# Moving a bias add ahead of the next tile's row split in a one-core SSM and mixture-of-experts kernel

## The reference, cut to what matters

```python
# x: 8 x 512 tokens x 256; first block: x + layernorm(S4D convolution block of layernorm(x))
def ffn(x, ...):                       # second block, 8 experts, 2 of them per token
    z = layernorm(x) * g + b
    probs = softmax(z @ rW + rb)
    w = the two largest probs, normalised to sum 1, zero elsewhere
    hid = gelu(z @ W1[e] + b1[e])      # 256 -> 512, every expert e
    outs = hid @ W2[e] + b2[e]         # 512 -> 256
    return x + sum over e of outs * w
x = x + layernorm(ffn(layernorm(x)))
```

## Time and profile before

| | us |
|---|---|
| median of 3 runs (lowest to highest) | 584.14 (581.31 to 586.74) |
| the profiled execution | 590.15 |
| its span, first to last instruction | 588.3 |
| TensorE busy, of the span | 479.5 (82%) |
| VectorE busy | 439.7 (75%) |
| ScalarE busy | 346.2 (59%) |
| GpSimd busy | 338.8 (58%) |
| mean granted clock of TensorE | 0.936 of full speed |

### The profile page before, as it was taken

The page is one execution under the profiler, slowest core; times in us unless marked ns, Lnnn a source line. Parts: engine busy times, 40 slices in busy tenths (PEclk is TensorE's granted clock), DMA queues, the critical chain, the costliest instruction groups (busy, mean ns, idle before and its releaser), DMA issues.

```text
span 588.3 us, 11874 instructions
## 1 busy us (share of the span) xinstructions
PE 479.5 (82%) x2775; PEld 393.4 (67%) x2775; DVE 439.7 (75%) x1468; ACT 346.2 (59%) x788; POOL 338.8 (58%) x266
## 2 busy tenths in 40 slices
PE   0297899968999974977699999999999999999200
PEld 0137888757889863543498888888888888888200
DVE  6999895999889875645677777777777777777183
ACT  6991854565676575812356555555555566556265
POOL 0000559533777883672247776767677676767457
PEclk9997999999999977979799999999999999999755
DMA  6304710051335548653544444444444444444497
GB/s 159 129 1 180 287 36 1 2 169 63 116 119 189 192 146 286 243 188 113 155 92 74 74 75 69 76 75 73 71 76 74 73 75 73 73 72 59 71 401 286
DMA packets 50161, 70.38 MB, mean 120 GB/s; under 512 B 10160, under 2 KB 39728, under 8 KB 49584
## 3 DMA queue, kind: packets, MB, share of 16 engines
q1 hardware_dynamic: 34528, 51.81, 27.1%
q0 software_dynamic: 15568, 17.81, 18.3%
HBM read 37.90 MB, written 31.69 MB: 118 GB/s over the span
## 4 chain that ended last, share of the span: by engine, by line
DVE 35%; ACT 19%; issue 17%; PE 14%; POOL 4%; DMA 4%; DVEq 3%; SPq 2%; ACTq 0%; POOLq 0%
DVE hb L1089 6%; ACT z_f L625 6%; ACT yw L648 4%; PE psum L1312 4%; DVE z_hl L1081 3%; DVE z_hl L1079 3%; POOL acc L1236 3%; DVEq L299 2%; DVE st L689 2%; DMA y_rows<-yw,dst 2%; PE psum L1283 2%; PE psum L1270 2%; DVE ws L883 2%; PE psum L1259 2%; PE psum L1260 1%
## 5 line engine op out<-in xcount | busy, mean ns | idle before, releaser
L1218 POOL DMA_INDIRECT y_rows<-yw,dst x71 | 115.9, 1632 | 54.5 <-DVE widx L1074 19.8
L1418 PE MATMUL psum<-ws,z_hl 128*128 x426 | 119.4, 416 | 1.1 <-DVE z_hl L1081 1.1
L1437 PE MATMUL psum<-ws,h_hl 128*128 x852 | 115.5, 285 | 0.1
L639 ACT ACTIVATE hg<-hb 128x512 f32<-128x512 f32 x71 | 44.9, 633 | 103.8 <-DVE hb L1089 81.1
L1437 PEld LDWEIGHTS psum<-ws,h_hl 128*128 128x128 f32 x852 | 103.2, 188 | 0.3 <-issue 0.3
L1205 POOL DMA_INDIRECT wt<-w_rows,widx x71 | 70.1, 988 | 44.5 <-issue 18.4
L1418 PEld LDWEIGHTS psum<-ws,z_hl 128*128 128x128 f32 x426 | 77.5, 189 | 16.1 <-issue 1.9
L1163 POOL DMA_INDIRECT z_rows<-zn,pos x64 | 68.8, 1074 | 28.7 <-issue 17.1
L1089 DVE TENSOR_TENSOR hb<-psum,b1r 128x512 f32<-128x512 f32 x71 | 49.1, 692 | 31.0 <-issue 29.4
L1312 PE MATMUL psum<-yf,it 128*128 128x256 f32 x256 | 59.9, 390 | 2.6 <-DVE r L932 2.6
L625 ACT ACTIVATE z_f<-psum,gb 128x128 f32<-128x128 f32 x142 | 56.0, 444 | 9.3 <-PE psum L1405 8.4
(11 more groups left out here) (204 smaller groups left out, 863.3 us busy)
## 6 DMA issues: line engine op xcount, KB each, us to landing
z_in<-z_rows SPq DMA_DIRECT2D x71, 129.0 KB
w_raw<-in_dram SPq DMA_DIRECT2D x16, 512.0 KB, 5.6
xs<-in_dram SPq DMA_DIRECT2D x8, 512.0 KB, 5.7
x_dram<-xs SPq DMA_DIRECT2D x8, 512.0 KB
y_rows<-zn SPq DMA_DIRECT2D x8, 512.0 KB, 3.2
yr<-y_rows SPq DMA_DIRECT2D x8, 512.0 KB, 6.5
out_dram<-acc SPq DMA_DIRECT2D x7, 512.0 KB, 4.7
b1r<-in_dram SPq DMA_DIRECT2D x8, 256.0 KB
```

Of the source, the lines that this page charges most:

```text
L1218: pool.indirect_dma_start(y_rows, bass.IndirectOffsetOnAxis(ap=dst[m][:, 0:1], axis=0), yw[m % 3][:, :], None, compute_op=ALU.add).then_in ...
L1418: last = TE.matmul(ps_h[q], z_hl[q][:, a, k], w_at(e1, c, k * F, F), start=n == 0, stop=n == 5)
L1437: last = TE.matmul(ps_y[q], h_hl[q][:, a, k], w_at(e2, c, 1024 + k * H, H), start=n == 0, stop=n == 11)
```

## The change

In VectorE's `part`, the bias add of tile i+1 goes from behind the split of tile i+2 to the head of the part. The load of an expert number, which stood ahead of that bias add and was for tile i+1, now stands ahead of the split and is for tile i+2; the bias add takes the register that the part before has loaded.

```diff
             def part(i, par, u):
+                t, q = i + 1, 1 - par
+                if live(t):
+                    e = expert(dve, t, u + 1)
+                    dve.wait_ge(sem("l1_mm"), t + 1)
+                    if not early(t):
+                        dve.wait_ge(sem("hg_ready"), t)
+                    V.tensor_tensor(hb[:, :], ps_h[q], b1r[:, bass.ds(e, 1)].rearrange("p a f -> p (a f)"),
+                                    ALU.add).then_inc(sem("hb_ready"), 1)
                 t, q = i + 2, par
                 if live(t):
...
                     V.tensor_tensor(widx[slot(t, u, 2) % 3][:, :], z_in[q][:, H:H + 1], flag[:, :],
                                     ALU.add).then_inc(sem("dest_ready"), 1)
+
+                    expert(dve, t, u + 2)
                     dve.wait_ge(sem("zf_ready"), t + 1)
...
                     V.tensor_tensor(z_hl[q][:, 1], z_f[:, :, :], z_hl[q][:, 0].bitcast(F32),
                                     ALU.subtract).then_inc(sem("z_split"), 1)
-                t, q = i + 1, 1 - par
-                if live(t):
-                    e = expert(dve, t, u + 1)
-                    dve.wait_ge(sem("l1_mm"), t + 1)
-                    if not early(t):
-                        dve.wait_ge(sem("hg_ready"), t)
-                    V.tensor_tensor(hb[:, :], ps_h[q], b1r[:, bass.ds(e, 1)].rearrange("p a f -> p (a f)"),
-                                    ALU.add).then_inc(sem("hb_ready"), 1)
                 t, q = i, par
                 if live(t):
                     dve.wait_ge(sem("h_high"), t + 1)
```

## The result

| | before | changed |
|---|---|---|
| median (lowest to highest), us | 585.22 (581.31 to 586.74), 4 runs | 653.96 (651.33 to 655.03), 4 runs |
| the profiled execution, us | 590.15 | 651.33 |
| ratio of changed to before, 95% interval | | 1.118 (1.111 to 1.125) |

The changed kernel is 11.8% slower; 646 us were forecast, within 628 to 664. The first place to look is the line of the bias add, whose first and last start bound the loop (answers to the earlier trace rows). The second line is the load of the expert number (answers to the earlier trace rows).

A forecast was written before the change was run, and what follows sets the result against it. It took the loop to be bound by a new chain, split, first-layer product, hb, next split: terms sum to 4.51 us a tile against 3.63, 0.88 more, 62 us over 70 periods, 584 + 62 = 646 us; range 628 to 664.

The forecast's parts named there:

- Step 1: VectorE, start of the new chain: hb to the next operation 0.61 us, `row_of` to `widx` 0.43 us.
- Step 2: VectorE, `widx` to the first half of the split, with the load between: 0.72 us, bounds 0.11 and 0.83.
- a rival of 4%: Load of the expert number slow at its new place: 0.26 us more a tile, 4.77 us and 664 us; 4%.
- Step 3: VectorE, first half of the split to its second half: 0.33 us.
- steps 3 to 5: Split halves 0.33 us; second half to weight load 0.57; first-layer product on TensorE 1.65; product's end to hb 0.20.
- The wait in front of hb: VectorE would stand 1.00 us a tile ahead of hb, until the first-layer product ends.
- TensorE's share in the loop: Sign of being right: TensorE's busy share in the loop falls to some three quarters.
- The load hides: Rival: the load runs during the wait for `flag`, period 3.90 us, time 603 us; 8%.
- hb is not kept waiting: Rival: product done when VectorE reaches hb, VectorE's row of 3.51 us sets the period, 576 us; 4%.
- The clock falls: Rival: TensorE's pauses lower its clock, chain at least 1.29 us longer, 736 us or more; 3%.
- The rule on the load: Skill's floor of about 600 ns for a `tensor_load`: `widx` to split some 0.3 us longer, total near 667 us.
- TensorE's floor: TensorE's own need in the loop: 3.32 us a tile, 0.31 under the period, so at most 22 us to win.

The follow-up runs named there:

- e8: Changed kernel with GpSimd's scatter of tile t held back until hb of tile t+4 is done; 653.04 us, ratio 1.112.
- e1: Changed kernel with the load of the expert number moved from between `widx` and the split to directly behind hb; 606.73 us, ratio 1.037.
- e4: Changed kernel with three of the six first-layer matmuls left out; 598.52 us, ratio 1.021.
- e5: Kernel before with three of the six first-layer matmuls left out; 585.21 us, ratio 0.999.
- e2: Kernel before with only the load moved, from directly ahead of hb to directly behind it; 569.79 us, ratio 0.976.
- e3: Kernel before with only the load moved, to between `widx` and the split, for one tile more ahead; 576.51 us, ratio 0.985.

## Why the prediction was right, step by step

The mechanism was right, and so were the sign, the range and the order of size. Of the steps, for the mean of the tiles from 300 to 600 us:

- Step 1, hb to the next operation and `row_of` to `widx`: 0.61 + 0.43 forecast, 0.61 + 0.44 measured.
- Step 2, `widx` to the split: 0.72 forecast, 0.84 measured. This is the term that was mis-sized. Its make-up was right: with the DMA engines idle it is 0.72 to 0.73 us, and with the scatter moved (e8) 0.74 in the mean. What the forecast didn't see is that a load which begins in a certain stretch behind a scatter's start is held up, and that the new order puts it there: 43 of the changed kernel's 70 loads behind the first began in it, and 3 of the kernel before's. That is 70 x 0.12 = 8 us, the size of what the forecast lacks; the rest nearly cancels. The row for it stood in the trace of before: a maximum of 562 ns beside a median of 304, which was put on an early tile and made a rival of 4%. It was no early tile but the 23rd load of 71, and it began 2.16 us behind a scatter's start:

```profile
364.68 1.58 POOL L1218 DMA_INDIRECT y_rows<-yw,dst  x1 [2.40 <-SPq L416]
```

```profile
L299 DVEq TENSOR_LOAD <-tab x1: 562/562/562, 366.8 to 366.8; - x1
```

- Step 3, half to half 0.33 forecast and 0.34 measured; steps 3 to 5 from the second half to hb 2.42 forecast and 2.38 measured. In the tile shown the product took 1.68 us against 1.65, and from its end to hb it was 0.13 us against 0.20: the second wait that was put there cost nothing that shows.
- The wait in front of hb: 1.00 us forecast, 0.96 measured. The sum: 4.51 forecast, 4.60 measured, and 4.51 in e8.
- TensorE's share in the loop: some three quarters forecast, 81% counted (40.58 of 50 us). Its work of 3.45 us in 4.60 would be 75%; the profile counts more; its ends of matmuls are modelled.

The rivals. "The load hides" would have given 603 us, and e1, where the load is really hidden, took 606.7. "hb is not kept waiting" is refuted by the wait itself, and e4 and e5 show that the product is what it waits for. "The clock falls": the granted clock stayed at 1.00, 2.4 GHz, in every 50 us from 300 to 600 us although TensorE's matmuls paused some 0.9 us in each tile. The Trainium skill (TensorE: Matmul & The Clock Gate, section "A second HAM failure mode: psum-queue depth-cycling") tells of a kernel whose pauses between groups of matmuls made the clock swing; the trace of this one shows no swing in that stretch.

The rule on the load (the Trainium skill, DMA: Bandwidth & Descriptors, section "Latency and other measured facts", a floor of about 600 ns for a `tensor_load`) is not borne out as a floor: 299 ns was the shortest of 71 and 394 the middle one. The load was slower than the trace of before said, and the total came between the two figures, but that is chance: e8 shows that the scatter made it slow, and without it the load takes 303 ns in the middle.

One step of the argument was wrong without harm to the number: TensorE's floor, 3.32 us forecast, 3.45 in e2. The 22 us that were put as the most to be won were therefore too many; e2, with nothing but TensorE left in its chain, won 16.

The whole loss of 68 us divides as follows, with the load where it hides as the base (569.8 us, e2): hb ahead of the split costs 37 us (e1 less e2), the load between `widx` and the split another 47 us (changed less e1). The kernel before pays 16 us for the load at its old place, directly ahead of hb, so 37 + 47 - 16 = 68. The two prices depend on each other: in the old order the load between `widx` and the split costs only 7 us (e3 less e2), and by that way round the order costs 77 us (changed less e3).

## What to carry to other kernels

In a software pipeline that one in-order engine both feeds and drains, moving the consumer of a result ahead of the next producer takes a whole stage of lead away. Before such a move, write down the distance from the operation that releases the other engine to the one that waits for it, in work of the engine in between: here 1.42 us stood against a path of 2.42 (2.38 measured). A register load on a busy engine had its best place in this kernel directly behind a long operation of that engine, where it runs beside it; e2 gained 2.4% with that alone. And a maximum far above the median is worth opening: its place in the trace can tell what it will meet in the new order.

## What the runs showed of the hardware that was not expected

- A load of one number from SBUF into a VectorE register took 303 ns in the median of the 583 loads that began outside the stretch of 1.89 to 2.36 us behind the start of GpSimd's scatter, and 477 ns, up to 649, in that of the 117 inside it. Busy DMA engines alone did not slow it: 155 loads outside the stretch with a DMA share of 0.6 or more took 304 ns in the median, 339 at most.
- In e1, at the same load, `row_of` started 0.66 us after hb in the median instead of 0.61: of about 0.6 us of load and register work, all but 0.05 us ran beside an operation of 0.69 us.
- TensorE's weight loads run ahead of its matmuls: 0.27 us of idle time in the weight loads, left out, made the tile only 0.13 us shorter (3.59 to 3.46, e2).
